# Experts' input turned through DRAM, a late scale, and two loads in another order, in a fused eight-batch block

## The reference, cut to what matters

```python
x = x + tanh(g_xattn[0]) * linear_attention(layernorm(x), ctx, Wq, Wg, bg, Wkv, Wo)   # stage A
x = x + tanh(g_ffn[0])   * (gelu(layernorm(x) @ proj1.T + b1) @ proj2.T + b2)         # stage F, hidden 2048
y = layernorm(x)                                                                       # "L"
x = x + tanh(g_xattn[1]) * softmax(mask(y @ ctx.T / sqrt(512))) @ ctx
z = layernorm(x)                                                                       # "M"
w_tg = top-8 of softmax(z @ gate_weight.T), normalised, summed by merge group          # 8 group weights a token
act = silu(z @ gate_g) * (z @ up_g)                                                    # 8 groups x 192
x = x + tanh(g_ffn[1]) * sum_g w_tg[:, g] * (act_g @ down_g)                           # stage E
```

## Time and profile before

| | |
|---|---|
| median of the runs | 1887.38 us |
| the profiled execution | 1887.08 us |
| its span, first to last instruction | 1885.3 us |
| TensorE busy | 1835.1 us, 97% |
| VectorE, ScalarE, POOL busy | 53%, 27%, 17% |
| stage F, from its first product | 397 to 1068 us |
| stage E | 1068 to 1885 us |
| one batch of stage E with the next one's attention beside it | 101.7 us |

### The profile page before, as it was taken

The page is one execution under the profiler, slowest core; times in us unless marked ns, Lnnn a source line. Parts: engine busy times, 40 slices in busy tenths (PEclk is TensorE's granted clock), DMA queues, the critical chain, the costliest instruction groups (busy, mean ns, idle before and its releaser), DMA issues.

```text
span 1885.3 us, 24530 instructions
## 1 busy us (share of the span) xinstructions
PE 1835.1 (97%) x9496; PEld 898.4 (48%) x9496; DVE 993.5 (53%) x2036; ACT 499.9 (27%) x745; POOL 319.3 (17%) x299
## 2 busy tenths in 40 slices
PE   8699999999999999999999899999999999999999
PEld 3445555544444444444444444444444444545444
DVE  5666776754555455453536463635455454546322
ACT  2324433411221221222112222222222232322211
POOL 1123322312012020202100011111111111111111
PEclk9999999999999999999999999999999999999999
DMA  4123433333323333230301210202020202011010
GB/s 158 55 63 129 140 118 99 92 129 79 101 68 104 108 79 110 63 99 11 90 31 32 74 42 18 76 24 70 22 77 12 87 12 67 33 41 28 18 50 29
DMA packets 145174, 129.01 MB, mean 68 GB/s; under 512 B 76642, under 2 KB 93154, under 8 KB 145058
## 3 DMA queue, kind: packets, MB, share of 16 engines
q1 hardware_dynamic: 145058, 127.45, 22.9%
HBM read 94.78 MB, written 32.64 MB: 68 GB/s over the span
## 4 chain that ended last, share of the span: by engine, by line
PE 81%; issue 8%; DVE 4%; DMA 3%; POOL 2%; ACT 1%; SPq 0%; POOLq 0%; DVEq 0%; ACTq 0%
PE bank L951 43%; PE bank L1040 16%; PE bank L1120 11%; PE bank L1020 4%; PE bank L960 3%; PE bank L1005 1%; PE bank L986 1%; POOL arena L925 1%; DMA arena<-group_weights 1%; DVE arena L1306 1%; PE bank L1055 1%; PE bank L1082 1%; POOL arena L899 0%; DMA arena<-in_L_xattn_Wkv 0%; DVE arena L1373 0%
## 5 line engine op out<-in xcount | busy, mean ns | idle before, releaser
L951 PE MATMUL bank<-arena 128*128 128x512 f16 x4608 | 1046.0, 380 | 9.0 <-DVE arena L1327 7.9
L951 PEld LDWEIGHTS bank<-arena 128*128 128x128 f16 x4608 | 449.7, 98 | 530.7 <-DVE arena L1327 8.3
L1040 PE MATMUL bank<-arena 128*128 128x512 f16 x1536 | 353.5, 380 | 5.4 <-DVE arena L1534 5.4
L1120 PE MATMUL bank<-arena 128*128 128x512 f16 x1152 | 265.7, 380 | 5.8 <-POOL arena L925 5.8
L1040 PEld LDWEIGHTS bank<-arena 128*128 128x128 f16 x1536 | 150.3, 98 | 186.5 <-DVE arena L1534 6.3
L1219 ACT ACTIVATE arena<-bank,arena 128x512 f32<-128x512 f32 x128 | 99.6, 778 | 489.3 <-PE bank L951 479.0
L925 POOL TENSOR_TENSOR arena<-arena 128x512 f16<-128x512 f32 x96 | 110.9, 1155 | 679.8 <-ACT arena L1256 658.3
L1532 DVE TENSOR_SCALAR arena<-arena 128x512 f16<-128x512 f32 x128 | 73.7, 576 | 273.9 <-ACT arena L1219 273.9
L1676 DVE SCALAR_TENSOR_TENSOR arena<-bank,arena 128x512 f32<-128x512 f32 x96 | 71.9, 749 | 273.3 <-PE bank L951 273.3
L1120 PEld LDWEIGHTS bank<-arena 128*128 128x128 f16 x1152 | 112.9, 98 | 140.1 <-POOL arena L925 6.8
L1256 ACT ACTIVATE arena<-arena 128x512 f16<-128x512 f32 x96 | 60.4, 629 | 377.9 <-DVE arena L1688 377.9
(11 more groups left out here) (159 smaller groups left out, 1146.6 us busy)
## 6 DMA issues: line engine op xcount, KB each, us to landing
arena<-in_L_ffn_proj SPq DMA_DIRECT2D x64, 256.0 KB, 3.0
arena<-group_weights SPq DMA_DIRECT2D x64, 256.0 KB, 3.3
arena<-in_L_ffn_gate_up_proj SPq DMA_DIRECT2D x96, 96.0 KB, 2.0
x_after_attention<-arena SPq DMA_DIRECT2D x8, 1024.0 KB, 5.2
arena<-x_after_attention SPq DMA_DIRECT2D x8, 1024.0 KB, 5.6
x_after_ffn<-arena SPq DMA_DIRECT2D x8, 1024.0 KB, 4.3
arena<-x_after_ffn SPq DMA_DIRECT2D x8, 1024.0 KB, 7.8
arena<-in_x SPq DMA_DIRECT2D x7, 1024.0 KB, 5.5
```

What stands on the lines that cost most here:

```text
L951: m = e.matmul(bank[b][:, :], wT[l][:, c, tile * P:(tile + 1) * P], y[h][:, c, :], start=n == 0, stop=n == NPASS - 1)
L1040: m = e.matmul(bank[t][:, :], hv[h][:, 0, t * P:(t + 1) * P], w2T[l][:, j, :], start=j == 0 and i == 0, stop=j == NH - 1 and i == 2)
L1120: m = e.matmul(bank[t][:, :], hv[h][:, 0, t * P:(t + 1) * P], dnT[l][:, j, :], start=j == 0 and i == 0, stop=j == NR - 1 and i == 2)
```

## The change

The norm M is turned in blocks for all eight batches, and its `whole` steps make the low half on VectorE; those of stage F stay on POOL. `hscale` is put off by six more flushes. In the last batch of stage F, what is left in `side` is added ahead of the store of x, and the first `gload` of stage E too; the second `gload` comes between the two loads of x.

```diff
 def in_blocks(i):
     ph, b = i
-    return ph == "F" and b > 0
+    return ph == "M" or (ph == "F" and b > 0)
...
+    def after(k, f):
+        late.append(f if k == 0 else lambda: after(k - 1, f))
+
     def after_max(name):
...
         if name in ("2", "d"):
             add("half", name)
-            late.append(lambda: add("hscale", name))
+            after(6, lambda: add("hscale", name))
...
             if jd == NH - 1:
                 for t in range(NT):
                     add("res2", bd, t)
+                if bd == NB - 1:
+                    while side:
+                        f = side.pop(0)
+                        if f:
+                            f()
+                    add("gload", 0, 0)
                 add("xstore", "F", bd)
...
     add("xload", "E", 1)
+    add("gload", 0, 1)
     add("xload", "E", 2)
...
-                if gg * INTER >= j * P and (b == 0 or gg > 1):
+                if gg * INTER >= j * P and gg > 1:
                     add("gload", b, gg)
...
@@ def pool_program(e):
-            elif kind == "whole":
+            elif kind == "whole" and step[1][0] == "F":
...
@@ def vector_program(e):
+            elif kind == "whole" and step[1][0] != "F":
+                _, i, c = step
+                w.wait_ge(b_hi, n)
+                y_free(w, i)
+                hi, lo = y_of(i)
+                e.tensor_tensor(lo[:, c, :], yraw[:, c, :], hi[:, c, :], ALU.subtract).then_inc(b_lo)
```

## The result

The changed kernel takes 1943.86 us (median of four runs, 1940.99 to 1948.89) against 1887.39: a ratio of 1.0304, with a 95% interval of 1.0284 to 1.0324. Forecast were 1929, in a range of 1896 to 1954. The profiled execution has a span of 1939.2 us, 53.9 more than before.

What follows compares the result with a forecast made beforehand. TensorE was taken to bound the kernel, busy 97% of the span. Hold +65.8, transposes -14.1, late scales -11.2 and F to E +1 gave +41.5 on 1887.1: 1929 us, range 1896 to 1954.

Steps and rivals of the forecast that it cites:

- The hold on SP: Stage E, batches 0 to 6: group 4's `gload` waits behind store and block loads, idling TensorE at `dn` 6; +65.8 us.
- slow start: The next 12 matmuls after a TensorE idle time run slower than 2.75 us; 1.5 us added per batch at `dn` 6.
- U: The time at which `ue` 6 leaves TensorE in a batch of stage E; the forecast's steps count from it.
- hold: On SP, from the start of the last store to the first DMA behind the four block loads: 7.3 us.
- The landing: Group 4's `gload` behind the block loads takes 3.5 us from its start until `mix` 6 can start.
- The transposes: Turns of M leave TensorE, 32 in all, for block transposes hidden on VectorE: -14.1 us.
- The late scales: At `hscale` of "2" and "d", six flushes later, the waits for POOL and slow starts go: -11.2 us.
- From F to E: Where stage F goes into E: the `dn` 0 gap goes, x of batch 1 comes late; +1 us, ends -7 and +6.
- Rival 4: `whole` steps on VectorE hold up the router, 14 us on top: 1943 us; chance 0.18 together with rival 3, a longer hold.
- The first rival: The cover holds: group 4's `gload` lands before `dn` 6 needs it, or isn't held; 1863 us, chance 0.10.
- the cover: The 7.8 us of TensorE work between U and `dn` 6, which could hide the late group 4 `gload`.

Runs made afterwards that it cites:

- e1: The changed kernel with group loads 4 and 5 of each batch put into the plan at tile 4, ahead of M's block steps: 1862.25 us, 0.9865.
- e3: The changed kernel with M's four block loads one task later in the plan, behind the load of group 4 and ahead of group 5's: 1875.44 us, 0.9927.
- e4: As e1, with `hscale` added at the next flush as in the kernel before: 1876.73 us, 0.9932.
- e6: As e1, with the order of the first loads of stage E as in the kernel before: 1864.22 us, 0.9869.
- e9: The changed kernel with only two of M's four block loads, each as large as before: 1923.91 us, 1.0188.
- e5: As e1, with x of batch 1 of stage E loaded first at stage F's end, and what is left in `side` ahead of the residuals: 1856.8 us, 0.9832.

## Why the prediction was right

**The hold on SP: right in place and mechanism, short in size.** It came in batches 0 to 6, at `dn` 6 and nowhere else, and e1 and e3 show the place in SP's stream as its cause. The term was 65.8 us. Measured are idle times of 63.2 in sum (9.0 each, forecast 7.9), 14.3 more for the twelve matmuls behind them (2.0 each, forecast 1.5), and 0.6 in sum for `ge` 8 behind these (from `dn` 6 to `dn` 7 it is 9.1 to 10.6 us, and 7.77 in e1): 78 us. The span of e1 is 80.0 us shorter; the other 2.0 are at the first turn of batch 1, where the change idles 0.3 longer and has a slow start of 1.7 that e1 has not. By the steps, in the mean of the seven batches: store at U + 2.2 (forecast 2.25), hold 7.1 (7.3), from there to the start of `mix` 6 5.0 (3.5), `mix` to POOL's end 2.6 (2.6). The landing is the mis-sized step: I added 0.2 us to the median of the earlier trace rows for the block load ahead of it. And the slow start was put at 1.5 from three rows; here it costs 1.4 to 2.55. Its size does not follow the idle time: it is 2.55 behind 4.3 us in e4 and in e6, 2.3 in the mean behind 5.5 to 7.0 in e9, and e1 has none behind 3.73.

**The transposes: right.** A batch without the idle time takes 100.0 us, 1.7 less than before, and VectorE's 55 us in it hide their price.

**The late scales: right in sum, wrong in a reason.** TensorE's idle times are gone and e4 brings them back, for 14.5 us. But at "d" the six flushes passed within about one product: VectorE still waits 4.77 us for POOL. TensorE is spared because the halves of one more product were made ahead of that wait.

**From F to E: right.** Idle 1.77 and 4.00 us and a slow start, against 1.3 and 5.5 forecast. e6 shows what the sum said, that the order of the change moves the lateness from the group load to x; the order of e5, which was not forecast, takes away most of both.

**Sum.** 78.1 - 14.1 - 11.2 + 0.3 = +53.1, where the span grew by 53.9. Rival 4's time of 1943 is that of the result, but not its mechanism: TensorE has no idle time at the router. The first rival, 1863, is what e1 measures once the cover is real.

The Trainium skill, page "DMA: Bandwidth & Descriptors", section "Anatomy of one DMA", says that a semaphore wait of a DMA is held on the issuing sequencer, ahead of dispatch. The trace agrees: in the changed kernel the group load starts 0.04 us after the last block load ahead of it in the plan, and not before.

## What to carry to other kernels

A queue that issues DMAs in order is a resource like an engine: before a wait is put into it, list what stands behind and when each of these is needed, for a load that was early by 34 us can become late by 9 through one place in a list. Put loads whose sources are ready ahead of a store, wait and reload chain. A change that is 56 us slower may be 27 faster with two steps moved, so time its parts apart.

## What the runs showed of the hardware that was not expected

Block loads of half the rows (128 KB on 16 partitions, in runs of 32 numbers) landed 5.6 us after their start at the median in the batches of stage E, up to 7.1, and those of 256 KB on 32 partitions 4.3, up to 5.8, though the halves were issued in about half the time (0.67 us each instead of 1.34 at the median). Half the bytes landed later, not sooner. Which part of the path sets that isn't settled here.

An idle time of TensorE of 3.73 us was followed by a product at full speed (e1), one of 4.00 in the changed kernel by a product of 4.44 us instead of 2.75, and the loss behind longer ones did not grow with them.
